# An attention and mixture-of-experts kernel: PE's lumps cut small and spread over the slots, q and k through the ring of shifted scores, straight code

## Chip, cores and metric

The kernel runs on one core of one Trainium2 chip. The metric is the device time of one execution in microseconds. Engines: PE is TensorE, DVE VectorE, ACT ScalarE, POOL GpSimd, SP SyncE (it only issues DMAs here).

## What is computed

One transformer layer on 16 batches of 256 tokens with 128 features, all in float32: attention with 16 heads of 8 features, then a mixture of 8 experts (top 2) and a shared expert.

```python
q, k, v = x @ Wq.T + bq, x @ Wk.T + bk, x @ Wv.T + bv      # 16 heads of 8
attn = softmax(q k^T / sqrt(8)) * head_mask
x = layernorm(x + (attn v) @ Wo.T + bo)
# routed: the two best of 8 experts per token, gates renormalised
y = shared(x) + sum over the two of gate_e * (gelu(x @ Wfc_e + bfc_e) @ Wproj_e + bproj_e)
out = layernorm(x + y)
```

## The kernel before

The attention (`build_attention`) is a pipeline over batches. In step t, PE, DVE, ACT, POOL and SP work on up to four batches at once: `new` = t, `now` = t-1, `late` = t-2, `last` = t-3. There are 19 steps; steps 0 to 3 and 14 to 18 are straight code, steps 4 to 13 run in a loop of five passes of two steps on each engine (`run_steps`, `Fori`). Steps 3 to 16 have work of all kinds but for the first and last batches' ends.

What a batch goes through. PE projects q and k (lines 588 and 589) into the PSUM bank `misc_ps`; ACT copies them out with the bias (370); POOL splits them in float16 parts (304, 306); SP writes the parts to rows in HBM (255 to 259) and reads them back, band by band, in `q_stack` and `k_stack` (225, 226). In the next step PE makes the scores of each head (527; 24 rows of the array, two tiles a head) in `s1_ps`, which has two places, and DVE takes the row maxima (443). POOL splits the maxima (292 to 296), PE turns them (569, in `misc_ps`), ACT copies them out (361), and SP adds them as two more rows to `q_stack` (215), in two halves of heads. In the step after, PE makes the shifted scores (543; 26 rows), two heads to a place of `st_ps`, which has two places, and ACT takes the exponentials into `probs` (354). `probs` has four buffers of a pair each. A quad (561) multiplies the probabilities of four heads with v: 8 float32 matmuls of 128 rows and 32 columns, which the trace shows as 16 instructions. One step later follow the copy out (380), the turning of `av` (622), the division by the sums and the head mask (465 to 472, DVE), the turning of the heads (628), the out projection (641), the addition of x (489), the statistics (493, 496), 1/sqrt on POOL (336 to 342), and the scaling to x1 on ACT (414).

A step of PE has 16 slots, one per head. In a slot PE issues four score matmuls: two tiles of `now`'s scores and two of `late`'s shifted scores. Between the slots stand the lumps: slot 0 q and k; slot 2 the maxima of the second half and quad 3 of `last`; slot 3 v; slot 5 the turning of `av`; slot 8 the heads; slot 11 the maxima of the first half; slot 13 the out projection; behind slots 6, 10 and 14 quads 0, 1 and 2 of `late`. All engines run their instructions in the written order; waits are on semaphores. In SP's order of a step, the second half's maxima come first, then x_t, x_in, the rows out, the stacks and the first half's maxima.

In step 18 PE turns rows for the routing stage between its slots (845). Then follow routing, the shared expert with the scattering of rows by POOL (886), the routed experts (39 blocks) and the last normalisation. Their loops take four tiles a pass; the first eight tiles are straight code.

Of the kernel before, what the change touches and what calls it, by code (L numbers as in the profile page):

```python
# [32 lines left out]
TURN_STEP = BATCHES + 2  # L33
TURNS = {1: (0, 1), 4: (2, 3), 7: (4, 5), 9: (6,)}
# [4 lines left out]
PASSED = [None]  # L39


class Batch:


    def __init__(self, u, c, back):
        self.half = u + (c - back) // 2
        self.par = (c - back) % 2
        self.n = self.half * 2 + self.par
        self.fixed = isinstance(u, int)

    def exists(self):
        return not self.fixed or 0 <= self.n < BATCHES

    def since(self, n):

        return not self.fixed or self.n >= n


def wait_first(eng, semaphore, value):


    eng.wait_ge(semaphore, value)
    if not isinstance(value, int):
        eng.sem_inc(PASSED[0], 1)


def run_steps(eng, step):

    for t in range(2 * FIRST_LOOP):
        step(t // 2, t % 2)  # L70
    with eng.Fori(FIRST_LOOP, FIRST_LOOP + LOOPS) as u:
        step(u, 0)
        step(u, 1)
    for t in range(2 * (FIRST_LOOP + LOOPS), BATCHES + 3):
        step(t // 2, t % 2)


def build_attention(nc, a):

    ctx = ExitStack()  # L80
    with ctx:
# [17 lines left out]
        wo = sb("wo", [D, D])  # L99
        bq = sb("bq", [D, 1])  # L100
# [3 lines left out]
        mask_row = sb("mask_row", [P, HEADS])  # L104
# [22 lines left out]
        probs = sb("probs", [P, 4, 2, TILES, SEQ])  # L127
        av = sb("av", [P, 2, SEQ])
        sum_inv = sb("sum_inv", [P, 2 * HEADS])
        sum_scale = sb("sum_scale", [P, 2 * HEADS])  # L130
# [6 lines left out]
        scaled_mean = sb("scaled_mean", [P, TILES])  # L137
        shift = sb("shift", [P, TILES])
# [3 lines left out]
        st_ps = ps("st_ps", [P, 2, 2, TILES, SEQ])  # L142
# [4 lines left out]
        misc16 = misc_ps[:].bitcast(F16)  # L147
# [13 lines left out]
        qk_projected = sem("qk_projected")  # L161
        qk_evacuated = sem("qk_evacuated")
# [9 lines left out]
        shifted_ready = sem("shifted_ready")  # L172
        exp_done = sem("exp_done")
# [18 lines left out]
        def _(sp):  # L192
            def load_xt(b):
                sp.dma_start(x_t[:, b.par], a["x_t"][:, bass.ds(b.n * SEQ, SEQ)]).then_inc(xt_in[b.par], 16)

            load_xt(Batch(0, 0, 0))
# [5 lines left out]
            sp.dma_start(mask_row[:], a["mask"].partition_broadcast(P)).then_inc(bcast_in, 16)  # L202
# [15 lines left out]
            def load_stacks(b, half):  # L218
                if b.since(2):

                    sp.wait_ge(shifted_ready, PAIRS * (b.n - 2) + (half + 1) * PAIRS // 2)
# [6 lines left out]
            def step(u, c):  # L228
                b = Batch(u, c, 2)
                if b.exists():  # L230
                    load_max(b, 1)
                b = Batch(u, c, -1)
                if b.exists():

                    if b.since(2):
                        sp.wait_ge(v_projected, b.n - 1)
                    load_xt(b)
                b = Batch(u, c, 2)
                if b.exists():
                    if b.since(2):  # L240
                        sp.wait_ge(xb_made, b.n - 1)
                    sp.dma_start(x_in[:, b.par], a["x"][bass.ds(b.n * SEQ, SEQ), :].rearrange("(t p) d -> p t d", p=P))\
                      .then_inc(x_loaded[b.par], 16)
                b = Batch(u, c, 0)
                if b.exists():


                    q_to = q_rows[b.par].rearrange("(r d) h t -> (d h) r t", r=TERMS)
                    k_to = k_rows[b.par].rearrange("(r d) h t -> (d h) r t", r=TERMS)
                    q_part, k_part = qk_parts[:, b.par, 0], qk_parts[:, b.par, 1]  # L250
                    if b.since(2):
                        for half in range(2):
                            sp.wait_ge(stacks_in[b.par][half], 64 * b.half)
                    sp.wait_ge(qk_split, 2 * b.n + 1)
                    sp.dma_start(q_to[:, 0:1], q_part[:, 0:1]).then_inc(rows_out[b.par], 16)
                    sp.dma_start(k_to[:, 2:3], k_part[:, 0:1]).then_inc(rows_out[b.par], 16)
                    sp.wait_ge(qk_split, 2 * b.n + 2)
                    sp.dma_start(q_to[:, 1:3], q_part[:, 0:2]).then_inc(rows_out[b.par], 16)
                    sp.dma_start(k_to[:, 0:2], k_part[:, 0:2]).then_inc(rows_out[b.par], 16)
                new, now = Batch(u, c, 0), Batch(u, c, 1)  # L260
# [7 lines left out]
                load_for_moe(sp, a, u, c)  # L268

            run_steps(sp, step)  # L270

        @block.gpsimd
        def _(pool):
# [9 lines left out]
            def split_max(b, half):  # L283
# [5 lines left out]
                wait_first(pool, max_done, HEADS * b.n + (half + 1) * HALF)  # L289
                if b.since(1):  # L290
# [17 lines left out]
            def step(u, c):  # L308
                b = Batch(u, c, 2)
                if b.exists():  # L310
                    split_max(b, 1)
# [1293 lines left out]
```

## Time and profile before

| | us |
|---|---|
| median of 3 runs | 655.3 |
| lowest, highest | 651.41, 659.56 |
| the profiled execution | 650.02 |
| its span | 648.3 |
| attention to the last out projection | about 334 |
| granted TensorE clock, mean of the span | 0.783 |

The profile is of one execution. Its span is the time from the first to the last instruction; the execution's own time is 1.7 us more. Times in the rows are from the span's start. The granted clock is 1.00 at 2.4 GHz and 0.50 at 1.2 GHz. Matmuls that run side by side on different rows or columns of the array, as a score and a shifted score or four matmuls of a quad, start within 0.01 us of each other, and PE's busy time counts them once. A matmul's duration holds its latency too, so two starts tell more than a duration.

### The profile page before, as it was taken

How to read it: one execution, taken by the hardware profiler on the slowest of the kernel's cores; microseconds unless marked ns; L12 is line 12 of the kernel's file. 1: busy time of each engine (PE TensorE's matmuls, PEld its weight loads, DVE VectorE, ACT ScalarE, POOL GpSimd, SP SyncE). 2: the span in 40 equal slices, each digit the busy share in tenths (PEclk: the TensorE clock that was granted, in tenths of full speed). 3: DMA queues.
4: the chain of work that ended last, by engine and by line, in shares of the span. 5: the costliest groups of instructions: out<-in, count | busy, mean ns of one | idle time of the engine just before them, and what ended most of it. 6: DMA issues, size and time to landing. Idle time of an engine off the chain costs nothing. (4 is left out here: it accounts for less than half of the span.)

```text
span 648.3 us, 15805 instructions
## 1 busy us (share of the span) xinstructions
PE 477.3 (74%) x5002; PEld 302.3 (47%) x5003; DVE 401.4 (62%) x871; ACT 306.2 (47%) x551; POOL 275.4 (42%) x398
## 2 busy tenths in 40 slices
PE   3898899988998989899961499800299999999000
PEld 2334344444344344434341399800188888888000
DVE  2757775666567576656558577600078888887066
ACT  1147755666556565644534477600054444443025
POOL 5203322323222232321024478877026677678366
PEclk9999975787578586855585599955599999999555
DMA  3222224242233423521205011111671011101093
GB/s 82 61 60 66 75 90 114 85 116 82 61 92 89 115 86 91 133 83 46 73 3 131 26 51 41 42 53 53 159 175 41 32 38 36 34 28 41 8 281 103
DMA packets 72502, 49.84 MB, mean 77 GB/s; under 512 B 9594, under 2 KB 65028, under 8 KB 72468
## 3 DMA queue, kind: packets, MB, share of 16 engines
q1 hardware_dynamic: 67924, 40.92, 23.2%
q0 software_dynamic: 4544, 8.47, 4.0%
q8 instruction: 20, 0.33, 0.2%
q14 instruction: 14, 0.11, 0.1%
HBM read 24.96 MB, written 22.95 MB: 74 GB/s over the span
## 5 line engine op out<-in xcount | busy, mean ns | idle before, releaser
L443 DVE TENSOR_REDUCE row_max<-s_ps 128x2 f32<-128x512 f32 x256 | 165.9, 684 | 98.0 <-PE s_ps L527 94.6
L354 ACT ACTIVATE probs<-st_ps 128x1024 f32<-128x1024 f32 x128 | 129.3, 1024 | 54.2 <-PE st_ps L543 53.4
L527 PE MATMUL s_ps<-k_stack,q_stack 24*128 24x256 f16 x512 | 113.9, 338 | 24.2 <-DVE row_max L443 11.4
L1306 POOL DMA_INDIRECT results<-gated,dest x78 | 89.2, 1144 | 64.1 <-DVE gated L1409 48.1
L1380 ACT ACTIVATE hid_r<-h_ps_r,bias 128x256 f32<-128x256 f32 x156 | 61.1, 474 | 114.7 <-PE h_ps_r L902 114.7
L543 PE MATMUL st_ps<-q_stack,k_stack 26*128 26x256 f16 x512 | 112.4, 339 | 0.4 <-ACT probs L354 0.4
L561 PE MATMUL av_ps<-probs,v_aug 128*32 128x256 f32 x1024 | 97.0, 513 | 0.0
L527 PEld LDWEIGHTS s_ps<-k_stack,q_stack 24*128 24x128 f16 x512 | 37.3, 104 | 101.5 <-DVE row_max L443 50.8
L886 POOL DMA_INDIRECT slots<-rows,slot_at x64 | 70.3, 1099 | 32.1 <-issue 18.9
L914 PE MATMUL y_ps_r<-w,hid_r 128*128 x312 | 59.0, 221 | 0.0
L915 PE MATMUL y_ps_r<-w,hid_r 128*128 x312 | 58.6, 219 | 0.0
L913 PE MATMUL y_ps_r<-w,hid_r 128*128 x312 | 58.1, 220 | 0.0
L292 POOL TENSOR_SCALAR max_scaled<-row_max 128x16 f32<-128x16 f32 x32 | 6.5, 205 | 114.0 <-DVE row_max L443 113.0
L1332 PE MATMUL t_ps<-ident_h,w_or_slots 128*128 128x128 f16 x156 | 17.4, 227 | 47.6 <-DMA w_or_slots<-slots 45.1
L561 PEld LDWEIGHTS av_ps<-probs,v_aug 128*32 128x32 f32 x1024 | 33.0, 134 | 35.5 <-issue 29.5
L1420 DVE SCALAR_TENSOR_TENSOR hid_r<-hid_r 128x1024 f16<-128x1024 f32 x39 | 48.1, 1232 | 1.3
L336 POOL TENSOR_SCALAR var_eps<-mean_var 128x2 f32<-128x2 f32 x16 | 3.5, 222 | 100.0 <-DVE mean_var L496 100.0
L900 PE MATMUL h_ps_r<-rows,w 128*128 128x256 f16 x156 | 43.6, 280 | 2.3 <-DVE rows L1399 2.3
L901 PE MATMUL h_ps_r<-rows,w 128*128 128x256 f16 x156 | 43.6, 279 | 0.0
L902 PE MATMUL h_ps_r<-rows,w 128*128 128x256 f16 x156 | 43.5, 279 | 0.0
L543 PEld LDWEIGHTS st_ps<-q_stack,k_stack 26*128 26x128 f16 x512 | 38.0, 106 | 8.0 <-issue 3.3
L1417 DVE TENSOR_SCALAR hid_r<-hid_r 128x1024 f16<-128x1024 f32 x39 | 27.1, 694 | 21.1 <-ACT hid_r L1380 19.9
(173 smaller groups left out, 1011.3 us busy)
## 6 DMA issues: line engine op xcount, KB each, us to landing
slots<-empty_row SPq DMA_DIRECT2D x6, 780.0 KB, 6.0
expert<-results SPq DMA_DIRECT2D x16, 256.0 KB, 5.1
w_or_slots<-slots SPq DMA_DIRECT2D x3, 1040.0 KB, 11.0
q_stack<-q_rows SPq DMA_DIRECT2D x64, 48.0 KB
k_stack<-k_rows SPq DMA_DIRECT2D x64, 48.0 KB
w_or_slots<-in_w_fc SPq DMA_DIRECT2D x9, 256.0 KB, 2.8
w_or_slots<-in_w_proj SPq DMA_DIRECT2D x9, 256.0 KB, 2.8
x_t<-in_x_t SPq DMA_DIRECT2D x16, 128.0 KB, 2.2
```

The costliest lines, as they stand in the source:

```text
L354: nc.scalar.activation(probs[:, p % 4], st_ps[:, p % 2], ACT.Exp, scale=SCORE_SCALE).then_inc(exp_done, 1)
L443: nc.vector.tensor_reduce(row_max[:, h], s1_ps[:, h % 2], AX_X, ALU.max, negate=True).then_inc(max_done, 1)
L527: mm = nc.tensor.matmul(s1_ps[:, h % 2, t], band_of(q_stack, b, h, TERM_ROWS)[:, t * P:(t + 1) * P], band_of(k_stack, b, h, TERM_ROWS), st ...
L543: mm = nc.tensor.matmul(st_ps[:, p % 2, n % 2, t], band_of(k_stack, b, h, rows)[:, t * P:(t + 1) * P], band_of(q_stack, b, h, rows), start ...
L561: mm = nc.tensor.matmul(av_ps[32 * j:32 * j + 32, r], v_aug[:, b.par, t, s * HALF + r * 4 + j], probs[:, (2 * n + j // 2) % 4, j % 2, t], ...
L886: nc.gpsimd.indirect_dma_start(out=a["slots"][:, :], out_offset=bass.IndirectOffsetOnAxis(ap=slot_at[:, k, t:t + 1], axis=0), in_=rows[:, ...
L913: nc.tensor.matmul(y_ps, h_hi[:, units], one_of(w16[:, 0], e, lo, hi), start=False, stop=False)
L914: nc.tensor.matmul(y_ps, h_hi[:, units], one_of(w16[:, 1], e, lo, hi), start=False, stop=False)
L915: mm = nc.tensor.matmul(y_ps, h_lo[:, units], one_of(w16[:, 0], e, lo, hi), start=False, stop=(c == CHUNKS - 1))
L1306: nc.gpsimd.indirect_dma_start(out=a["results"][:, :], out_offset=bass.IndirectOffsetOnAxis(ap=dest[:, t.buf, half:half + 1], axis=0), in_ ...
L1380: act_ = nc.scalar.activation(hid[:, t.buf % 2, cols], h_ps[:, t.buf % 2, cols], ACT.Gelu_apprx_tanh, scale=1.0 / UNIT, bias=bias[:, t.buf ...
L1420: nc.vector.scalar_tensor_tensor(out=hid16[:, t.buf, 1], in0=hid[:, t.buf % 2], scalar=X_UNIT, in1=hid16[:, t.buf, 0], op0=ALU.mult, op1=A ...
```

## The change

- A quad is cut in two half quads (4 matmuls each, one tile of probabilities). PE's lumps now stand: slot 0 k; 1 half quad 2b of `last`; 2 maxima, half quad 3a; 3 half quad 3b; 4 v; 6 turning of av; 7 and 8 quad 0; 10 maxima, 1a; 11 1b; 12 heads; 13 half quad 2a; 14 out projection; 15 q of the batch ahead. All stand ahead of the slot's scores.
- q and k are projected into the ring of two places that the shifted scores use; a batch's q and k take one place, and the ring has nine fillings a step.
- `probs` has six buffers; the exp of a pair waits for a quad one pair older than before.
- The head mask is multiplied once into `wo_masked`; the operation on `sum_scale` goes.
- x1 is scaled on POOL with (z - mean) * rstd; `scaled_mean`, `shift` and ACT's scaling go. The statistics of a batch are taken one step later, so there are 20 steps.
- SP sends the rows of q and k ahead of x_t and x_in.
- All loops, in the attention and behind it, are straight code; `wait_first` with its extra increments goes.

The diff, cut to its core:

```diff
+STEPS = BATCHES + 4
+PROBS = 6
-        with eng.Fori(FIRST_LOOP, FIRST_LOOP + LOOPS) as u: ...
+def run_steps(step):
+    for t in range(STEPS):
+        step(t)
+def ring_order():
+    at = {("qk", 0): 0}
+    for t in range(STEPS):
+        if Batch(t - 2).exists():
+            for p in range(PAIRS):
+                at["pair", t - 2, p] = len(at)
+        if Batch(t + 1).exists():
+            at["qk", t + 1] = len(at)
+    return at
...
 SP, step:
+                if late.exists():
+                    load_max(late, 1)
+                if new.exists():
+                    send_rows(new)
+                if ahead.exists():
+                    load_xt(ahead)
...
 POOL:
+            def make_x1(b):
...
+                nc.gpsimd.tensor_tensor(rstd[:], var_eps[:], minus_half[:], ALU.pow).then_inc(scale_done, 1)
+                pool.wait_ge(scale_done, 2 * b.n + 2)
+                for t in range(TILES):
+                    nc.gpsimd.tensor_scalar(x1_all[:, b.n * TILES + t], z[:, t], mean_var[:, t, 0:1], rstd[:, t:t + 1],
+                                            ALU.subtract, ALU.mult).then_inc(x1_made, 1)
+            # order: split_max(late, 1), split_qk(new), make_x1(gone), add_bias(last), split_max(now, 0)
 ACT:
-                if b.since(1) or p >= 4:
-                    act.wait_ge(quad_done, 4 * b.n + p // 2 - 1)
+                if n >= PROBS:
+                    act.wait_ge(quad_done, (n - PROBS) // 2 + 1)
+            # order: evacuate_qk(new), pair 0, max(late, 1), pair 1, av(last), v(now), pairs 2 3 4,
+            #        max(now, 0), pair 5, heads(last), pairs 6 7
 DVE:
+            # order: maximum 0, stats(gone), maximum 1, mean(gone), maxima 2 to 7, sums and division(last),
+            #        maxima 8 to 15, add_residual(last)
+            nc.vector.tensor_tensor(wo_masked[:], wo[:], mask_col[:].to_broadcast([D, D]), ALU.mult)
 PE:
+            def half_quad(b, n, t):
...
+                for j in range(4):
+                    mm = nc.tensor.matmul(av_ps[32 * j:32 * j + 32, r], v_aug[:, b.par, t, s * HALF + r * 4 + j],
+                                          probs[:, (PAIRS * b.n + 2 * n + j // 2) % PROBS, j % 2, t], start=(s == 1 and t == 0),
+                                          stop=(s == 0 and t == 1))
+            def project_q(b):
+                key = ("qk", b.n)
+                pe.wait_ge(xt_in[b.par], 16 * (b.half + 1))
+                if place[key] >= 2:
+                    pe.wait_ge(ring_emptied, filled(key) - 2)
+                nc.tensor.matmul(ring(key)[:, 0, 0], wq[:], x_t[:, b.par], start=True, stop=True)
+            def project_k(b):
+                nc.tensor.matmul(ring(("qk", b.n))[:, 0, 1], wk[:], x_t[:, b.par], start=True, stop=True).then_inc(ring_filled, 1)
...
+                    if slot == 0 and new.exists():
+                        project_k(new)
+                    if slot == 1 and last.exists():
+                        half_quad(last, 2, 1)
+                    if slot == 2 and late.exists():
+                        if gone.exists():
+                            pe.wait_ge(z_made, gone.n + 1)
...
+                        turn_max(late, 1)
+                    if slot in (2, 3) and last.exists():
+                        half_quad(last, 3, slot - 2)
...
+                    if slot in (7, 8) and late.exists():
+                        half_quad(late, 0, slot - 7)
...
+                    if slot == 14 and last.exists():
+                        project_out(last)
+                    if slot == 15 and ahead.exists():
+                        project_q(ahead)
 behind the attention:
-    with eng.Fori(2, loop_end) as u: ...
+    for s in range(steps):
+        step(s // 4, s % 4)
```

## Rows read from the trace of the kernel before

**Rows 1.** The page, part 1: busy us, share of the span and instructions.

```profile
PE 477.3 (74%) x5002; PEld 302.3 (47%) x5003; DVE 401.4 (62%) x871; ACT 306.2 (47%) x551; POOL 275.4 (42%) x398
```

**Rows 2.** Busy time by stretch: steps 3 to 16, routed experts. Columns: stretch, length, engines, clock, DMA.

```profile
46.90:308.60 261.70, 234.35 (x2072) 108.99 (x2071) 171.06 (x337) 155.47 (x248) 68.59 (x180) 0.74 0.32 89
...
470.00:602.00 132.00, 124.52 (x1619) 112.89 (x1617) 107.48 (x230) 61.10 (x156) 85.92 (x75) 0.99 0.18 52
```

**Rows 3.** Busy time by step: steps 4, 6 and 9 (PE, PEld, DVE, ACT, POOL, clock).

```profile
62.70:78.30 15.60, 12.99 (x148) 6.20 (x148) 11.91 (x25) 11.18 (x18) 4.64 (x14) 1.00 0.25 71
...
96.10:118.70 22.60, 21.75 (x151) 9.79 (x149) 12.42 (x24) 11.41 (x18) 5.02 (x13) 0.50 0.31 83
...
152.10:174.40 22.30, 20.41 (x151) 9.19 (x149) 12.53 (x25) 11.29 (x18) 5.62 (x15) 0.56 0.24 71
```

**Rows 4.** Busy time by stretch of one granted clock, four of sixteen.

```profile
49.00:89.90 40.90, 34.03 (x395) 16.11 (x395) 31.84 (x62) 29.43 (x48) 13.16 (x32) 1.00 0.29 85
89.90:120.70 30.80, 29.95 (x204) 13.64 (x197) 16.90 (x35) 15.51 (x24) 6.97 (x20) 0.50 0.26 71
...
154.80:175.30 20.50, 19.65 (x138) 9.02 (x139) 11.30 (x23) 9.55 (x15) 4.39 (x10) 0.50 0.23 68
...
270.80:328.90 58.10, 54.58 (x384) 24.43 (x382) 33.90 (x69) 29.36 (x43) 9.11 (x28) 0.50 0.28 78
```

**Rows 5.** Timeline of PE in step 6, half clock, to its end. Columns: start, us, what.

```profile
105.56 0.42 PE L543 MATMUL st_ps<-q_stack,k_stack 26*128 26x256 f16 x1
...
105.77 0.42 PE L543 MATMUL st_ps<-q_stack,k_stack 26*128 26x256 f16 x1
...
106.11 1.94 PE L561 MATMUL av_ps<-probs,v_aug 128*32 128x256 f32 x16
...
106.55 0.20 PEld L561 LDWEIGHTS av_ps<-probs,v_aug 128*32 128x32 f32 x4 [0.23 <-issue]
...
107.98 0.39 PE L527 MATMUL s_ps<-k_stack,q_stack 24*128 24x256 f16 x1
...
114.15 1.22 PE L641 MATMUL misc_ps<-wo,heads_t 128*128 128x128 f32 x4
115.30 0.39 PE L527 MATMUL s_ps<-k_stack,q_stack 24*128 24x256 f16 x1
...
116.27 1.94 PE L561 MATMUL av_ps<-probs,v_aug 128*32 128x256 f32 x16
...
118.67 1.22 PE L588 MATMUL misc_ps<-x_t,wq 128*128 128x256 f32 x2
...
120.68 0.28 PE L527 MATMUL s_ps<-k_stack,q_stack 24*128 24x256 f16 x1
```

**Rows 6.** Groups of instructions by line: busy us, mean ns, idle before.

```profile
L414 ACT ACTIVATE x_all<-z,shift,rstd 128x128 f32 (+1 forms) x32 | 13.9, 483 | 4.0 <-POOL shift L342 3.9
...
L304 POOL TENSOR_SCALAR qk_parts<-qk 128x512 f16<-128x512 f32 x16 | 9.9, 617 | 21.3 <-ACT qk L370 21.3
...
L292 POOL TENSOR_SCALAR max_scaled<-row_max 128x16 f32<-128x16 f32 x32 | 6.5, 205 | 114.0 <-DVE row_max L443 113.0 <-issue 0.9
```

**Rows 7.** Timeline of SP's DMA issues in step 4, full clock.

```profile
66.46 2.69 SPq L215 DMA_DIRECT2D q_stack<-max_t  x4
69.46 0.39 SPq L194 DMA_DIRECT2D x_t<-in_x_t  x1
...
70.80 0.33 SPq L255 DMA_DIRECT2D q_rows<-qk_parts  x1
...
75.85 2.72 SPq L215 DMA_DIRECT2D q_stack<-max_t  x4
```

**Rows 8.** Timeline of PE at slot 0 of step 15.

```profile
268.94 0.27 PE L527 MATMUL s_ps<-k_stack,q_stack 24*128 24x256 f16 x1 [1.70 <-DMA q_stack<-max_t]
```

**Rows 9.** Timeline of PE: the q projections of steps 2 and 4.

```profile
27.58 1.22 PE L588 MATMUL misc_ps<-x_t,wq 128*128 128x256 f32 x2
...
62.69 0.69 PE L588 MATMUL misc_ps<-x_t,wq 128*128 128x256 f32 x2
```

More of the change, by code:

```diff
@@ L36, with __init__ @@
 FIRST_LOOP, LOOPS = 2, 5
-PASSED = [None]
 class Batch:
[L45 to L49, printed above, removed]
-    def exists(self):
[L52 to L75, printed above, removed]
+    def __init__(self, n):
+        self.n = n
+        self.par = n % 2
+        self.half = n // 2
+    def exists(self):
+        return 0 <= self.n < BATCHES
+def ring_order():
[10 more added lines that the diff above has]
+        step(t)
 def build_attention(nc, a):
@@ new lines, in step @@
+            def step(t):
+                ahead, new, now, late = (Batch(t - back) for back in range(-1, 3))
+                if late.exists():
[4 more added lines that the diff above has]
+                    load_xt(ahead)
+                if late.exists():
+                    if late.n >= 2:
+                        sp.wait_ge(xb_made, late.n - 1)
+                    sp.dma_start(x_in[:, late.par], a["x"][late.n * SEQ:(late.n + 1) * SEQ, :].rearrange("(t p) d -> p t d", p=P))\
+                      .then_inc(x_loaded[late.par], 16)
@@ new lines, in step @@
+            def step(t):
+                new, now, late, last, gone = (Batch(t - back) for back in range(5))
+                if late.exists():
+                    split_max(late, 1)
+                if new.exists():
+                    split_qk(new)
+                    if new.n == 0:
+                        make_routing_constants(nc, pool, a)
+                if gone.exists():
+                    make_x1(gone)
+                if last.exists():
+                    add_bias(last)
+                if now.exists():
+                    split_max(now, 0)
@@ L566, in turn_max @@
-            def turn_max(b, half):
-                rows = MAX_PARTS * HALF * TILES
-                wait_first(pe, max_split, (2 * b.n + half) * 3 + 3)
-                nc.tensor.transpose(misc16[0:rows, 0:P], max_parts[:, half].rearrange("p r n -> p (r n)"), ident16[:])\
-                  .then_inc(max_turned, 1)
-            def step(u, c):
-                new, now, late, last = (Batch(u, c, back) for back in range(4))
-                turning = isinstance(u, int) and 2 * u + c == TURN_STEP
+                if t == 0:
+                    pe.wait_ge(ring_emptied, emptied(("pair", b.n, 2 * n + 1)))
+                    if n == 0:
+                        pe.wait_ge(v_evacuated, 2 * b.n + 2)
+                        if b.n >= 1:
+                            pe.wait_ge(av_evacuated, b.n)
+                        else:
+                            pe.wait_ge(bias_made, 1)
@@ L576, in step, with project_out @@
+            def project_out(b):
+                pe.wait_ge(heads_evacuated, b.n + 1)
+                for t in range(TILES):
+                    mm = nc.tensor.matmul(half_ps[:, t * D:(t + 1) * D], heads_t[:, t * P:(t + 1) * P], wo_masked[:],
+                                          start=True, stop=True)
+                mm.then_inc(y_ready, 1)
+            def step(t):
+                ahead, new, now, late, last, gone = (Batch(t - back) for back in range(-1, 5))
                 for slot in range(HEADS):
-                    if turning:
+                    if t == TURN_STEP:
@@ L604, in step @@
+                    if slot == 4 and now.exists():
+                        if now.n == 0:
+                            pe.wait_ge(weights_in, 64)
                         if late.exists():
                             pe.wait_ge(max_evacuated, 2 * late.n + 2)
[L606 to L610 removed]
@@ L611, in step @@
-                        mm.then_inc(v_projected, 1)
-                    if slot == 5 and last.exists():
+                        project_v(now)
+                    if slot == 6 and last.exists():
                         if now.exists():
```

504 lines of the change are left out of this document (218 added, 286 removed).

## The prediction

> **What bounds the kernel now.** I read the page's busy shares first, then the busy times by stage, by step of the attention, by stretch of one granted clock, and then single instructions. PE is the busiest engine and is busy for three quarters of the span [rows 1]. The change touches the attention above all, whose fourteen full steps (3 to 16) fill 46.9 to 308.6, 261.7 us [rows 2]. These steps do the same work and don't take the same time: 15.6 us at clock 1.00, 22.6 us at 0.50 [rows 3]. In the first PE is busy for 12.99 us, DVE 11.91 and ACT 11.18, so no engine is full; in the second PE is busy 21.75 of 22.6 and nothing else matters. The reader should see two kernels in one: a latency-bound one at 2.4 GHz and a PE-bound one at 1.2 GHz.
>
> How the steps are shared out follows from the stretches of one clock [rows 4] (sixteen of them from 5 us on). From 46.9 to 308.6 the full-clock ones add up to 122.6 us (7.9 steps of 15.6) and the half-clock ones to 139.1 us (6.2 steps of 22.6), which gives the 0.74 of [rows 2]. Ahead of 49 us the row's 1.00 isn't to be believed: a q projection took 1.22 us at 27.58 as it does at half clock, against 0.69 at 62.69 [rows 9]. The kernel starts at half clock.
>
> **What moves the clock here.** A full PE doesn't raise it: from 89.9 PE was busy 29.95 of 30.8 us at 0.50, from 270.8 it was busy 54.58 of 58.1 us and stayed at 0.50 [rows 4]. Each of the seven rises in the attention (49.0 to 253.8) comes in the first 7 us of a step. There the work on the whole array (128*128, or four 128*32 side by side) stands densest: quad 2 (116.27), one slot of scores, q and k without a break (118.67 to 120.68), then quad 3, v and the transposes; at 120.7 the clock rises [rows 4, 5]. The 58 us in which it never came back are the ones in which no q/k projection ran at half clock, since the last ran at 266.1. The falls (89.9, 137.7, 154.8, ..., 270.8) come behind scores on 24 or 26 of the 128 rows and a stall, as the 1.70 us at 268.94 [rows 8]. So whole-array work packed together goes ahead of a rise, and mere occupation doesn't bring one. This is read from when things happen; it isn't proven.
>
> **The change on PE, at half clock.** One pair of score matmuls takes 0.21 us (105.56 to 105.77), a slot of two pairs 0.43. A quad starts 0.13 us after the last pair has streamed (106.11 - 105.77 - 0.21), its four groups are 0.43 or 0.44 apart (106.11, 106.55), and the next scores start at 107.98, 0.16 us behind 4 x 0.43. A quad costs 1.71 + 0.29 = 2.00 us, 0.29 of it edges [rows 5]. A half quad costs 0.86 + 0.29 = 1.15. Eight for four quads: 8 x 1.15 - 4 x 2.00 = +1.2 us a step. The out projection costs 0.13 + (115.30 - 114.15) = 1.28; q and k together cost 0.13 + (120.68 - 118.67) = 2.14, and apart, in slots 15 and 0, 2 x 1.28: +0.4 us [rows 5]. Against that, stalls that lumps of 2 us cause shrink; the step has 0.85 us without PE busy [rows 3], of which I take 0.4 back. 22.6 + 1.6 - 0.4 = **23.8 us** per half-clock step. The bounds are 22.9 (edges half as dear, since the next weights may be loaded ahead) and 24.6 (no stall returned and an edge of 0.35).
>
> More important is the order. At half clock the new PE runs lump, slot of scores, lump, slot of scores from slot 13 to slot 4. Between two score slots stands at most 0.86 us of whole-array work, in 1.15 + 0.43 = 1.58 us. The old stretch that led to the rise at 120.7 had 1.71 (quad) + 1.71 (q and k) = 3.4 us of it in the 4.4 us from 116.27 to 120.68 [rows 5]. Nothing as dense is left anywhere: q has a slot of scores between itself and k, and every quad is cut. The start is no help either: step 0 has q, k and the small bias matmul together, as before, and that didn't raise the clock before [rows 9]. I therefore take it that the clock, which starts at 0.50, isn't raised before the turning step, where transposes of the routing stage run without scores.
>
> **The rest, part by part.** *x1 on POOL*: ACT loses 2 x 0.48 us a step (line 414); POOL gets two scalings of 128x128, between the 0.205 of 16 elements and the 0.617 of 512 [rows 6]; by length 0.30 each, 0.6 us, and loses two small ones of about 0.2. POOL is busy 4.6 to 5.6 us a step [rows 3]: hidden. Its queue holds split_max(now, 0) behind make_x1 and add_bias; both are done long before slot 8's maximum. The scaling gates DVE's next addition to z one step later: hidden. *Mask in the weights*: one DVE operation less a step, one 128x128 multiply once: DVE has over 10 us free at half clock. *Six probs buffers*: exps wait for a quad one pair older; only full-clock steps could gain. *q/k through the ring*: nine fillings a step in two places where there were eight; an ACT that is busy 11.4 of 22.6 us covers them. Its cost falls on full-clock steps, where a pair's scores wait for the evacuation of q and k (0.9 us); nothing to 0.5 us. *turn_max in slot 2* waits for the z of the batch before, now the last thing DVE does in a step; two slots and a k projection at half clock (over 2 us) cover 0.42 us of z. *SP*: rows go ahead of x_t and x_in. In a full-clock step SP issues the second half's maxima at 66.46, x_t at 69.46, rows at 70.80, and the next maxima, which slot 0 waits for, from 75.85 to 78.57 [rows 7]. Taking x_t and x_in out of that order shortens it by 70.80 - 69.46 = 1.3 us, so a **full-clock step** would go from 15.6 to 14.3, I say 14.4; at half clock it is slack. *Step 19*: the last batch's statistics come one step later, with nothing between; the ACT scaling (0.97) becomes 0.6 of POOL. -1 to +1. *Straight code*: behind 339 us PE in the routed stage is busy 124.52 of 132 us [rows 2], so loops and register arithmetic have little to give: 0 to -3, I take -1; more instructions to fetch, nothing in the steps that were already straight shows a cost: 0 to +3. Routing, shared expert, routed experts and the last normalisation are as before.
>
> **The sum.** Steps 3 to 16 at half clock: 14 x 23.8, less the q of step 15 and the q and k of step 16 (3 x 1.28), is 329.4 us against 261.7: **+67.7**. Steps 2, 17 and 18, at half clock before and after, have two, four and two lumps more: +2. Tail and code: -2. 650.0 of the profiled execution (span 648.3) becomes 718. The median of the runs lies 5.3 us above that execution; with it, **722**. Bounds by 22.9 and 24.6 a step: 705 to 735.
>
> **The rivals.**
> *The clock rises and stays (faster).* Place: any half-clock window that brings it up. From there the same evenness keeps it up: at 2.4 GHz a slot with a lump would last about 0.9 us, whole-array work comes in nearly every slot, and only slots 5 and 9 are left with scores alone. Price: 14 x 14.4 = 202 for 261.7, -60: 595. It pays for itself as soon as about 48% of the steps run at full clock (23.8 against 14.4, mean 18.7). For it: at full clock PE would be busier than the 12.99 of 15.6. Against it: it has to rise first, and a wait of 1.7 us for maxima at slot 0 would end it, with no way back.
> The Trainium skill, page "TensorE: Matmul & The Clock Gate", the section on the HAM clock gate, says of throttling that "the default state is throttled, and activity releases the throttle"; by that rule a PE that never idles would be released, and the time would be this rival's 595. The trace doesn't agree: 54.58 busy of 58.1 us at 0.50 [rows 4].
> I give it 0.14 from the start of the full steps and 0.12 for a rise on the way, 600 to 642.
> *Alternation as before (no change).* 7.9 x 14.4 + 6.2 x 23.8 = 261: gain at full clock and loss at half cancel, 655. So also if the DMA order eats the gain. For it: my reading rests on seven rises. 0.12.
> *My forecast*: 0.62.
>
> **How the numbers follow.** Two per cent is about what a measurement of this kernel tells from no change. Slower by more: 0.62. Within: 0.12. Faster: 0.14 + 0.12 = 0.26. The range goes to 735 above; below it has to reach into the faster cases until no more than 0.2 is left out: 615 leaves the 0.14 at 595 and a little of the way there. The likeliest case's own range is 705 to 735.
>
> **What would show it.** Right: granted clock 0.50 nearly throughout from 50 to about 395 us, steps near 23.8 us with PE busy over 95%, quads as x8 groups 1.15 us wide from scores to scores, DVE's waits for scores grown; DVE and ACT busy times less by about 3 and 15 us. Wrong: a stretch at 1.00 longer than 60 us. If steps are 14 to 15 us, the clock was what I misread; if half-clock steps are under 22.6, the edges were.

## The result and the profile after

The changed kernel takes 704.96 us (median of four runs, 704.37 to 705.75), the kernel before 657.43 on the same chip (651.41 to 660.08): a ratio of 1.0737, 95% interval 1.0655 to 1.082. The forecast was slower, 722 us. Ratios given with an interval leave out runs over 1.5% above the fastest run of their kernel, so they can differ a little from the quotient of the medians.

First the page of the changed kernel: busy time by engine, then the three rows in 40 slices that matter.

```profile
span 702.6 us, 14097 instructions
...
PE 559.1 (80%) x5002; PEld 303.0 (43%) x5002; DVE 403.5 (57%) x855; ACT 293.5 (42%) x519; POOL 285.9 (41%) x398
...
PE   3899999999999999999999616994007999999200
...
PEclk9999999999999999999999857998557999999755
```

Against [rows 1], PE is busy 82 us more with the same 5002 instructions. No work was added to it, so each instruction lasts longer. The groups by line say which (line, engine, operation, tile, count | busy us, mean ns | idle before):

```profile
L531 PE MATMUL s_ps<-k_stack,q_stack 24*128 24x256 f16 x512 | 147.2, 404 | 3.6 <-DVE row_max L437 1.9 <-issue 0.4
L547 PE MATMUL ring_ps<-q_stack,k_stack 26*128 26x256 f16 x512 | 146.6, 405 | 0.0
L565 PE MATMUL av_ps<-probs,v_aug 128*32 128x256 f32 x1024 | 138.8, 631 | 0.7 <-ACT probs L350 0.7
```

One score matmul is recorded with 404 ns on the mean. At half clock [rows 5] record 0.39 to 0.42 us, at full clock the traces record 0.27 or 0.28 (further down), and a mix of both had to give something between. So the scores ran at half clock throughout. The PEclk row prints 9 all the same: the first clock event in this trace stands at 391.0 us, and ahead of it the row shows full speed by default, as the prediction said of the first 49 us of the trace before [rows 9]. A reader who believed the row would look for the loss in the wrong place; durations decide.

Now the attention. Busy time of steps 3, 4, 5 and 14, and of steps 3 to 16 together (the clock column is that default); these answer to [rows 2, 3]:

```profile
47.90:71.00 23.10, 23.02 (x150) 8.07 (x148) 11.57 (x18) 10.43 (x16) 3.70 (x9) 1.00 0.16 48
71.00:94.10 23.10, 23.01 (x150) 8.07 (x148) 12.45 (x23) 10.44 (x16) 6.28 (x13) 1.00 0.17 47
94.10:117.20 23.10, 23.01 (x150) 8.07 (x148) 12.45 (x23) 10.44 (x16) 6.26 (x13) 1.00 0.24 70
302.20:325.30 23.10, 23.01 (x151) 8.06 (x149) 12.45 (x23) 10.44 (x16) 6.25 (x13) 1.00 0.31 82
47.90:368.20 320.30, 318.76 (x2074) 112.01 (x2076) 172.89 (x317) 145.24 (x222) 83.27 (x176) 1.00 0.27 74
```

From 47.90 to 325.26 each step takes 23.11 us, like a clock, with PE busy 23.01 of it. A kernel that alternated between latency-bound and PE-bound steps has become PE-bound in all of them. DVE and ACT have idle time for it: maxima wait 162.8 us for scores (94.6 in the page of before), the exps 193.8 us for theirs (53.4 before).

```profile
L437 DVE TENSOR_REDUCE row_max<-s_ps 128x2 f32<-128x512 f32 x256 | 173.0, 690 | 165.3 <-PE s_ps L531 162.8
L350 ACT ACTIVATE probs<-ring_ps 128x1024 f32<-128x1024 f32 x128 | 131.2, 1025 | 193.8 <-PE ring_ps L547 193.8
```

The order at half clock, slots 15 to 2 around the start of step 14 (start, us, what): q, k and two half quads, each with a slot of scores behind it. From the start of a lump to the next scores it is 1.3 us at most, here 1.02 to 1.30:

```profile
300.46 1.22 PE L581 MATMUL ring_ps<-x_t,wq 128*128 128x256 f32 x2
301.61 0.39 PE L531 MATMUL s_ps<-k_stack,q_stack 24*128 24x256 f16 x1
...
302.15 1.22 PE L584 MATMUL ring_ps<-x_t,wk 128*128 128x256 f32 x2
303.45 0.37 PE L531 MATMUL s_ps<-k_stack,q_stack 24*128 24x256 f16 x1
...
303.65 0.42 PE L547 MATMUL ring_ps<-q_stack,k_stack 26*128 26x256 f16 x1
303.99 1.08 PE L565 MATMUL av_ps<-probs,v_aug 128*32 128x256 f32 x8
305.01 0.39 PE L531 MATMUL s_ps<-k_stack,q_stack 24*128 24x256 f16 x1
...
305.55 1.13 PE L565 MATMUL av_ps<-probs,v_aug 128*32 128x256 f32 x8
306.62 0.39 PE L531 MATMUL s_ps<-k_stack,q_stack 24*128 24x256 f16 x1
```

Where the 54.3 us between the two spans lie: 1.0 ahead of step 3 (47.90 against 46.9), 58.6 in steps 3 to 16 (320.3 against 261.7), 3.2 from there to the first routing logit (at 402.20 against 339.35), and behind it -8.6.

### The profile page after: what moved, and what is told of

Its sections match the earlier page's. It is cut to its first block and busy times, and to the rows that moved or that the text cites. A ratio compares the mean times of both kernels' runs of the same rounds, so it can differ in the third digit from the quotient of the medians.

```text
span 702.6 us, 14097 instructions
## 1 busy us (share of the span) xinstructions
PE 559.1 (80%) x5002; PEld 303.0 (43%) x5002; DVE 403.5 (57%) x855; ACT 293.5 (42%) x519; POOL 285.9 (41%) x398
## 5 line engine op out<-in xcount | busy, mean ns | idle before, releaser
L437 DVE TENSOR_REDUCE row_max<-s_ps 128x2 f32<-128x512 f32 x256 | 173.0, 690 | 165.3 <-PE s_ps L531 162.8
L350 ACT ACTIVATE probs<-ring_ps 128x1024 f32<-128x1024 f32 x128 | 131.2, 1025 | 193.8 <-PE ring_ps L547 193.8
L531 PE MATMUL s_ps<-k_stack,q_stack 24*128 24x256 f16 x512 | 147.2, 404 | 3.6 <-DVE row_max L437 1.9
L547 PE MATMUL ring_ps<-q_stack,k_stack 26*128 26x256 f16 x512 | 146.6, 405 | 0.0
L565 PE MATMUL av_ps<-probs,v_aug 128*32 128x256 f32 x1024 | 138.8, 631 | 0.7 <-ACT probs L350 0.7
L1322 POOL DMA_INDIRECT results<-gated,dest x78 | 79.2, 1015 | 65.5 <-DVE gated L1423 52.4
L931 PE MATMUL y_ps_r<-w,hid_r 128*128 x312 | 58.2, 220 | 0.0
L932 PE MATMUL y_ps_r<-w,hid_r 128*128 x312 | 58.0, 219 | 0.0
L930 PE MATMUL y_ps_r<-w,hid_r 128*128 x312 | 57.7, 220 | 0.0
L565 PEld LDWEIGHTS av_ps<-probs,v_aug 128*32 128x32 f32 x1024 | 27.6, 142 | 41.3 <-issue 27.4
L547 PEld LDWEIGHTS ring_ps<-q_stack,k_stack 26*128 26x128 f16 x512 | 38.8, 112 | 7.9 <-issue 6.0
L1431 DVE TENSOR_SCALAR hid_r<-hid_r 128x1024 f16<-128x1024 f32 x39 | 27.1, 694 | 15.1 <-ACT hid_r L1394 15.1
L1409 DVE COPY bias<-b_units 128x4 f32 x39 | 7.1, 182 | 47.4 <-issue 47.4
```

Of the source, the lines that this page charges most:

```text
L350: nc.scalar.activation(probs[:, n % PROBS], ring(key), ACT.Exp, scale=SCORE_SCALE).then_inc(ring_emptied, 1)
L437: nc.vector.tensor_reduce(row_max[:, h], s1_ps[:, h % 2], AX_X, ALU.max, negate=True).then_inc(max_done, 1)
L531: mm = nc.tensor.matmul(s1_ps[:, h % 2, t], band_of(q_stack, b, h, TERM_ROWS)[:, t * P:(t + 1) * P], band_of(k_stack, b, h, TERM_ROWS), st ...
L547: mm = nc.tensor.matmul(ring(("pair", b.n, p))[:, n % 2, t], band_of(k_stack, b, h, rows)[:, t * P:(t + 1) * P], band_of(q_stack, b, h, ro ...
L565: mm = nc.tensor.matmul(av_ps[32 * j:32 * j + 32, r], v_aug[:, b.par, t, s * HALF + r * 4 + j], probs[:, (PAIRS * b.n + 2 * n + j // 2) % ...
L930: nc.tensor.matmul(y_ps, h_hi[:, units], one_of(w16[:, 0], e, lo, hi), start=False, stop=False)
```

## The experiments

Theories. **Order**: the sequence of PE's work decides whether the clock rises; whole-array work packed together goes ahead of a rise, and the new order has none. **Mere size**: the half quads' and ring's edges simply cost PE time. **Ring or waits**: the new dependences, not the clock, hold the steps. Each kernel below is set against runs of the kernel before ("before" for short) on its own chip.

**A burst of whole-array work.** Eight extra projections into a scratch tile, once, in step 3 ahead of the turning of the maxima:

```diff
+                        if t == 3:
+                            for _ in range(8):
+                                nc.tensor.matmul(misc_ps[:, 0:SEQ], wq[:], x_t[:, new.par], start=True, stop=True)
                         turn_max(late, 1)
```

> The kernel after, with eight extra 128x128 float32 matmuls (6.8 us at half clock, result unused) once, in step 3 ahead of the turning of the maxima. Theory (the clock starts at half and the evenly spread lumps never bring it up, while nothing else is wrong with the new order): the clock rises during or right behind the burst, and from there the same evenness keeps it up; steps of 14 to 15 us instead of 23.1, about 705 + 7 - 13 x 8.5 = 600 us; if a stall at slot 0 brings it down once, it is stuck again and the time is between 610 and 700. Rival (the new order costs PE time by itself, by its edges and waits): the burst adds its 7 us, 712 us.

Measured: median 697.19 us (three runs at 697.04 to 697.35, one at 656.54), before 661.59. The clock rose at 53.4 us, 2 us into the burst, which is 4.72 us long by its timeline, and 338 us earlier than in the changed kernel. It stayed up for 34.1 us, until 87.5, then was at half until 384.5. The burst, then the whole stretch at full clock, the one full step in it, and a later step at half (same columns as the tables of busy time before):

```profile
51.33 4.72 PE L633 MATMUL misc_ps<-x_t,wq 128*128 128x256 f32 x16
```

```profile
53.40:87.50 34.10, 28.68 (x301) 12.69 (x303) 22.72 (x41) 19.41 (x31) 7.56 (x19) 1.00 0.22 62
69.58:85.72 16.14, 13.43 (x151) 5.42 (x149) 12.23 (x23) 10.21 (x16) 6.30 (x13) 1.00 0.24 69
110.00:133.10 23.10, 23.01 (x152) 8.06 (x148) 12.44 (x23) 10.43 (x17) 6.27 (x14) 0.50 0.31 82
```

So half clock was no fault of the waits: with the clock up, the same order runs a step in 16.14 us instead of 23.11. But it is not the prediction's 14.4, and it doesn't hold the clock: the 600 us of the expectation were missed, and its other case, a fall that leaves the kernel stuck (610 to 700), came about. The fall came behind two waits on ACT, 0.27 us ahead of q and 0.61 us at the start of the next step:

```profile
84.79 0.67 PE L581 MATMUL ring_ps<-x_t,wq 128*128 128x256 f32 x2 [0.27 <-ACT probs L350]
87.02 0.26 PE L531 MATMUL s_ps<-k_stack,q_stack 24*128 24x256 f16 x1 [0.61 <-ACT probs L350]
...
87.34 0.97 PE L565 MATMUL av_ps<-probs,v_aug 128*32 128x256 f32 x8
```

The same two waits stand one step earlier (at 68.66 and 70.89) with no fall behind them, and PE was never idle for longer than 0.79 us while the clock was up. So the waits alone don't explain the fall. The run of 656.54 has no trace; its mean granted clock is 0.782 where the other three have 0.693. In it the clock stayed up longer or came back, so the order isn't a certain lock once the clock has moved.

**The same burst on 24 rows.** In the same place 32 matmuls of the scores' shape, 24 of the 128 rows, results unused:

```diff
+                        if t == 3:
+                            for _ in range(32):
+                                nc.tensor.matmul(misc_ps[:, 0:SEQ], q_stack[0:TERM_ROWS, now.par, 0, 0:P],
+                                                 k_stack[0:TERM_ROWS, now.par, 0], start=True, stop=True)
                         turn_max(late, 1)
```

> The same place and the same length of burst, but of 32 matmuls on 24 of the 128 rows (float16, 0.21 us each at half clock, result unused). Theory (whole-array work goes ahead of a rise, occupation doesn't): the clock stays at half, 705 + 7 = 712 us. Rival (any uninterrupted run of matmuls releases the clock): the same as the burst on the whole array, near 600.

Measured: 712.02 us (710.89 and 713.16), 1.0818 of before (1.0669 to 1.0967). First clock event at 397.8, routing at 408.93, 6.7 us later than in the changed kernel, which is about the burst itself:

```profile
51.23 7.03 PE L633 MATMUL misc_ps<-k_stack,q_stack 24*128 24x256 f16 x32
```

PE was occupied without a break for 7.0 us and nothing rose; 4.7 us on all rows raised it. PE is occupied in both, in the second even longer. But the two bursts differ in more than the rows: the first is float32, the second float16. The trace of the changed kernel answers this further on, in the routed experts. There PE ran float16 matmuls of the same width, on all 128 rows, from 531.05 on at half clock, and the clock rose at 534.35:

```profile
531.05 0.39 PE L917 MATMUL h_ps_r<-rows,w 128*128 128x256 f16 x1 [1.00 <-DVE rows L1413]
...
534.00 0.42 PE L917 MATMUL h_ps_r<-rows,w 128*128 128x256 f16 x1
534.22 0.34 PE L918 MATMUL h_ps_r<-rows,w 128*128 128x256 f16 x1
534.39 0.27 PE L919 MATMUL h_ps_r<-rows,w 128*128 128x256 f16 x1
```

So float16 work goes ahead of a rise too when it fills all rows, and the type isn't what held the second burst back. Bursts of one type on more and on fewer rows, in one place, were not run.

**Lumps packed again, the rest of the change kept.** Quads whole in slots 2, 7, 10 and 13, q beside k in slot 0:

```diff
                     if slot == 0 and new.exists():
+                        if new.n >= 1:
+                            project_q(new)
                         project_k(new)
-                    if slot == 1 and last.exists():
-                        half_quad(last, 2, 1)
-                    if slot in (2, 3) and last.exists():
-                        half_quad(last, 3, slot - 2)
+                    if slot == 2 and last.exists():
+                        half_quad(last, 3, 0)
+                        half_quad(last, 3, 1)
... quads 0, 1 and 2 likewise, whole in slots 7, 10, 13
-                    if slot == 15 and ahead.exists():
-                        project_q(ahead)
```

> The kernel after with PE's lumps packed as before: quads whole (slots 2, 7, 10, 13), q next to k in slot 0; ring, six buffers, x1 on GpSimd and straight code stay. Theory: the clock rises again at the beginning of steps and falls in between, 640 to 660 us. Rival (another part of the change costs the 47 us): 690 to 705, less the edges alone.

Measured: 634.27 us (630.41 to 639.91), 0.9617 of before (0.9512 to 0.9722), better than the 640 to 660 expected. It beats both kernels. The trace is of the longest run, 639.91. The clock rises nine times in the attention (74.3 to 326.9) and once stays up for 75.1 us. Two full-clock steps:

```profile
163.45:178.60 15.15, 12.37 (x149) 5.99 (x148) 11.77 (x24) 10.19 (x17) 6.27 (x13) 1.00 0.36 106
193.76:208.90 15.14, 12.36 (x149) 6.00 (x148) 11.76 (x24) 10.18 (x17) 6.28 (x13) 1.00 0.37 106
```

The first rise, at 74.3, came inside the quad of slot 2, behind q and k without a break and two slots of scores; the next scores already take 0.28 us instead of 0.39:

```profile
69.82 1.22 PE L581 MATMUL ring_ps<-x_t,wq 128*128 128x256 f32 x2
70.83 1.06 PE L584 MATMUL ring_ps<-x_t,wk 128*128 128x256 f32 x2
71.83 0.39 PE L531 MATMUL s_ps<-k_stack,q_stack 24*128 24x256 f16 x1
...
72.80 1.83 PE L565 MATMUL av_ps<-probs,v_aug 128*32 128x256 f32 x16
74.56 0.28 PE L531 MATMUL s_ps<-k_stack,q_stack 24*128 24x256 f16 x1
```

Six probs buffers, the ring, the mask in the weights, x1 on POOL and the DMA order are all still in this kernel. None of them by itself is the loss.

**Quads whole, q still in slot 15.**

```diff
 (against the packed kernel)
-                        if new.n >= 1:
-                            project_q(new)
                         project_k(new)
...
+                    if slot == 15 and ahead.exists():
+                        project_q(ahead)
```

> Quads whole again, but q still in slot 15 and k in slot 0. Theory: the edges of the half quads go (-1.2 us a half-clock step, 690 us at least), and the 1.7 us of a whole quad bring the clock up now and then: 650 to 690. Rival (only q and k side by side bring it up): 23.1 - 1.2 = 21.9 us a step throughout, 690 us.

Measured: 678.48 us (673.16 and 683.80) against 661.59. Seven short rises, 3.4 to 23.9 us. The half-clock step takes 22.98 us, hardly less than 23.11: the edges of four cuts that were saved come back as waits, for PE is busy only 21.77 of 23.00 us:

```profile
69.60:92.60 23.00, 21.77 (x152) 9.26 (x148) 12.05 (x23) 10.43 (x16) 6.29 (x13) 0.50 0.17 48
```

**q beside k, quads in halves.** The changed kernel with one lump moved:

```diff
                     if slot == 0 and new.exists():
+                        if new.n >= 1:
+                            project_q(new)
                         project_k(new)
...
-                    if slot == 15 and ahead.exists():
-                        project_q(ahead)
```

> The kernel after with q back in slot 0 beside k; the quads stay in halves. Theory: q and k together are 1.7 us of whole-array work without scores between, so the clock rises in some steps, less often than with whole quads as well: 640 to 680 us, half-clock steps 0.4 us shorter than 23.1. Rival (the cut quads alone keep the clock down): 14 x 0.4 less than 705, 698.

Measured: 693.84 us (679.61 to 700.04) against 709.22 for before; on this chip the stages behind the attention take about 60 us longer (from the first logit to the end 361 us against 300, 40 us of it up to the first routed transposition, 164 against 124), so ratios are compared. That of the medians is 0.978 here, but only one run of four is near the fastest, so it is rough. Routing begins at 328.71. The clock was up from 72.2 to 198.5 without a break. One full-clock step and two at half:

```profile
85.74:100.83 15.09, 13.12 (x149) 5.50 (x148) 12.14 (x24) 10.32 (x17) 6.29 (x13) 1.00 0.37 108
212.41:234.94 22.53, 22.53 (x149) 8.38 (x148) 12.36 (x24) 10.43 (x17) 6.27 (x13) 0.50 0.25 73
234.94:257.47 22.53, 22.53 (x150) 8.39 (x149) 12.35 (x24) 10.43 (x17) 6.27 (x13) 0.50 0.32 83
```

**Half quads alone, in the kernel before** (each quad's two tiles in two neighbouring slots, nothing else):

```diff
-                    if slot == 2 and last.exists():
-                        quad(last, 3)
+                    if slot in (2, 3) and last.exists():
+                        quad(last, 3, slot - 2)
...
-                        if slot in (6, 10, 14):
-                            quad(late, (slot - 6) // 4)
+                        if slot in (6, 7, 10, 11, 14, 15):
+                            quad(late, (slot - 6) // 4, (slot - 6) % 4)
```

> The kernel before with its quads in halves and nothing else (slots 2 and 3, and behind slots 6, 7, 10, 11, 14, 15); q and k stay together in slot 0. Theory: less whole-array work in one piece, so fewer rises, and 1.2 us more of edges in a half-clock step: 665 to 690. Rival (halves feed DVE more evenly and are worth it): 640 to 655.

Measured: 744.79 us (737.39 to 752.13), 1.0445 of before (1.0335 to 1.0555). In the trace, of the longest of the four runs, half clock held from 80.9 to 207.2 us, with steps like these:

```profile
80.90:207.20 126.30, 120.74 (x788) 47.55 (x785) 67.03 (x130) 60.94 (x96) 27.19 (x72) 0.50 0.26 71
88.30:111.90 23.60, 22.56 (x149) 8.87 (x148) 12.53 (x24) 11.42 (x18) 4.91 (x13) 0.50 0.23 68
```

Cutting the quads is enough to lose 4%, though q stands beside k here as well. Part of it is size and not clock: the half-clock step takes 23.60 us against 22.6, up to 1.0 us a step. So neither cut alone explains the result, and "q beside k" alone doesn't save it: where the other lumps stand around it counts too.

**Straight code alone, in the kernel before**, behind the attention, nothing else:

```diff
-    for s in range(8):
-        step(s // 4, s % 4)
-    with eng.Fori(2, loop_end) as u: ...
+    for s in range(steps):
+        step(s // 4, s % 4)
... the loops of PE and DVE over the routed blocks likewise
```

> The kernel before with straight code behind the attention alone; the attention keeps its loop. From the two traces the stages behind the attention took 309.0 us before and 300.4 after. If straight code did it: 8 us less than before in the same runs. If the indirect transfers or the clock of that execution did it: no difference.

Measured: 709.02 us against 709.22, 0.9974 (0.9909 to 1.0038): none of the 8 us, on the chip with the long stages. Read by its expectation this clears the straight code; the same kernel on a chip of the other kind, below, says otherwise.

**A hybrid**: q beside k, quads 2 and 3 whole, quad 0 cut between slots 7 and 9, quad 1 between 10 and 11.

```diff
 (against q beside k)
-                    if slot == 1 and last.exists():
-                        half_quad(last, 2, 1)
-                    if slot in (2, 3) and last.exists():
-                        half_quad(last, 3, slot - 2)
+                    if slot == 2 and last.exists():
+                        half_quad(last, 3, 0)
+                        half_quad(last, 3, 1)
-                    if slot in (7, 8) and late.exists():
-                        half_quad(late, 0, slot - 7)
+                    if slot in (7, 9) and late.exists():
+                        half_quad(late, 0, (slot - 7) // 2)
                     if slot == 13 and late.exists():
                         half_quad(late, 2, 0)
+                        half_quad(late, 2, 1)
```

> From the fully packed order (634 us): q and k together, quads 2 and 3 whole, but quad 0 in halves in slots 7 and 9 and quad 1 in halves in slots 10 and 11, because the packed order's falls came 7 to 11 us behind a step's start, behind slots of scores alone. Theory: rises as often, falls less often: 615 to 632 us. Rival (any cut makes rises rarer and that costs more): 640 to 665.

Measured: 699.90 us (689.90 to 700.89) against 709.22. Stretches at full clock of 3.4 to 23.9 us that alternate with falls; routing at 339.01. The theory (615 to 632 us, which is 0.93 to 0.96 of the 661.59 of the first experiments) failed: by medians the hybrid is 0.987 of before, no better than q beside k alone. The reading of rises and falls didn't tell beforehand which order keeps the clock up.

**The three orders side by side.** The changed kernel, q beside k, and the packed kernel once more, unaltered, on one chip (again one with the long stages):

> The changed kernel as it is, on the chip of the two runs below, so that the three stand side by side. If the order of the work sets the clock (my theory), attention steps of 23.1 us without a rise again, the routing stage begins about 402 us behind the start on a chip like the first, ratio to before 1.07. If the missing rise were an accident of one chip or one session, a stretch of full clock in the attention and under 690 us.

> q's projection beside k's in slot 0, the rest of the change as it is. By my theory this one move brings rises in the attention that the changed kernel lacks: on a chip like the first, router at about 330 to 340, ratio to before 0.96 to 0.98 and 0.90 to 0.92 of the changed kernel. By the rival, that the half quads alone keep the clock down, under 0.97 of the changed kernel isn't reached.

> Whole quads in slots 2, 7, 10 and 13 and q beside k in slot 0, the rest of the change as it is. 0.96 of before as in its first run. Against q beside k with half quads: if whole quads add rises, 5 to 15 us less than it; if the lump of q and k is what counts, the two are within 5 us of each other.

Measured, with before at 714.83:

| kernel | median us | of before (95%) | routing begins at |
|---|---|---|---|
| changed | 771.21 | 1.0805 (1.0723 to 1.0886) | 403.32 |
| q beside k | 703.18 | 0.9895 (0.9802 to 0.9988) | 330.88 |
| packed | 690.43 | 0.9682 (0.9596 to 0.9769) | 323.70 |

The changed kernel has its first clock event at 393.7 us, as on the first chip, so the lock is the kernel's and not a chip's. One projection moved by one slot gives 68 us back. The packed order is 12.8 us better than that by medians, but one of its four runs took 709.29, so I call the sign likely and the size open. Of before, q beside k reaches 0.9895 where 0.96 to 0.98 was expected; the 0.90 to 0.92 of the changed kernel holds (0.912).

Taken together, with the rest of the change kept and each on its own chip: packed 0.962 and 0.968 of before, only the quads cut 0.978 and 0.990, only q apart from k 1.026 (two runs), both 1.074 and 1.081. Here moving q away from k is the dearer of the two cuts.

**Straight code once more**, the same kernel as above:

> The kernel before with straight code behind the attention and nothing else, once more. The five profiles of straight code from the chip on which the shared expert takes about 50 us have the routed experts, from the first transposition to the last projection, at 128.2 to 128.8 us; the loops of before had 135.8. If the straight code is the cause of that difference, 128 to 129 us in this profile and 0.985 to 0.99 of before, where the chip is of that kind; if the attention's change is the cause, 135 to 136 us and no difference. On a chip of the other kind (shared expert about 130 us) I expect about 150 us either way, and nothing is told apart.

Measured: 649.28 us against 657.46, 0.9897 (0.9823 to 0.9972). This chip has the short stages. The routed experts, from the first transposition to the last projection: of the kernel before (loops), of the changed kernel, and of this one:

```profile
463.00:599.00 136.00, 128.19 (x1638) 115.30 (x1638) 107.95 (x233) 61.10 (x156) 83.53 (x73) 0.97 0.24 66
```

```profile
526.70:655.30 128.60, 122.66 (x1638) 113.56 (x1638) 106.75 (x233) 61.22 (x156) 74.44 (x74) 0.97 0.26 72
```

```profile
466.20:594.20 128.00, 122.42 (x1637) 113.48 (x1638) 106.84 (x233) 61.22 (x156) 73.76 (x74) 0.97 0.26 72
```

The 128 us come with the straight code and not with the attention's change. From the first logit to the end of the span this kernel takes 300.7 us, the changed one 300.4, the kernel before 309.0: nearly all of the -8.6 us is the straight code's.

## Why the prediction was right, and where its sums were off

**The likeliest case came about as argued.** The clock starts at half and isn't raised before the turning step: first event at 391.0, where the prediction put "about 395". PE is busy 23.01 of 23.11 us. The time itself, 704.96, lies at the very edge of that case's own range (705 to 735), since the errors below nearly all run one way. The share of the full-clock steps was the whole question, and the reading of [rows 4, 5], which was marked as unproven, has since been tested: the bursts on all rows and on 24 rows, and the three orders. What is shown is that in this kernel the order decides and that occupation doesn't. What exactly raises or keeps the clock isn't: half quads beside q and k keep it up for 126.3 us in one kernel and down for 126.3 us in another. Nor are the falls explained.

On the Trainium skill, page "TensorE: Matmul & The Clock Gate", Part 1, the text says that a monitor sets the clock "based on how busy the PE has been recently". The runs don't agree if busy means occupied: 318.76 of 320.3 us at half clock, and a rise only where all rows worked.

**The half-clock step: 23.11 us, forecast 23.8** (bounds 22.9 to 24.6). Its two parts were both a little off. PE's busy time grew from 21.75 to 23.01, by 1.26 where 1.6 was summed. The price of a half quad isn't the reason: on the chip it is (303.99 - 303.65 - 0.21) + (305.01 - 303.99) = 1.15 us, as summed. Where the other 0.34 went stays open. And the idle 0.85 us of the old step shrank to 0.10: 0.75 came back where I took 0.4. Even work is better at removing stalls than I allowed; it just isn't worth it at half clock. Steps 3 to 16 took 320.3 us, forecast 329.4: +58.6 for +67.7. In the terms of the sum: 718 was forecast for a profiled execution that took 704.4; 9.1 of the difference are these steps, 6.6 the straight code (below), and the steps around them took 2.2 more than summed. The 5.3 us from profile to median of the kernel before had no counterpart: the changed kernel's runs lie within 1.4 us. So the theory of mere size is answered too: cutting and moving the lumps costs 0.5 us a half-clock step (23.11 against 22.6 before; 22.98 with whole quads, 22.53 with q beside k), at most 14 x 0.5 = 7 us of the 58.6. In the kernel before the cut quads cost 1.0 (23.60).

**Steps ahead and behind.** +2 for steps 2, 17 and 18; measured 1.0 ahead of step 3 and 3.2 between step 16 and the logits, with step 19 in it: +4.2, and step 19 had been given -1 to +1.

**Straight code.** -1 was taken from 0 to -3; it is -8.6 in the traces, on chips of the one kind. The step of the argument that failed is that PE in the routed stage "is busy 124.52 of 132 us [rows 2], so loops and register arithmetic have little to give". In these 136 us PE's busy time fell from 128.19 to 122.66 with the same count of matmuls: busy time itself held something the loops cost. On the chip with long stages the routed experts take 149.93 us straight, and 150.85 in the one trace with loops there (that of the half quads alone); why the gain isn't seen on that chip is open. What it is that overlaps better in straight code isn't shown.

**The full-clock step: 14.4 forecast, wrong.** The changed order has 16.14, where before had 15.6. The maxima's DMAs, which slot 0 waited for, hold neither the full step of the burst nor the one of q beside k any more. But the term was too large: 1.3 us was what SP's issues would shrink by, while PE's wait for them in the step that was priced, step 4 of before, is 0.68, and no more could come back:

```profile
64.50 0.28 PE L527 MATMUL s_ps<-k_stack,q_stack 24*128 24x256 f16 x1 [0.68 <-DMA q_stack<-max_t]
```

In its place stand, in the step of the burst, ACT (0.79 us for `v_aug`, 0.45 and 0.61 for `probs`, 0.27 ahead of q) and POOL (0.59 for `max_parts`). The 0.61 and the 0.27 stand where q and k, one ring place filled in two different slots, meet the exps; with q beside k neither is in the trace and the step is 15.09. I had given this "nothing to 0.5"; it is about 1. These are the waits of the full-clock step of q beside k, to compare:

```profile
91.48 0.66 PE L596 MATMUL misc_ps<-ident,av 128*128 128x128 f32 x4 [0.79 <-ACT v_aug L373]
...
95.12 0.22 PE L573 MATMUL misc_ps<-ident,max_parts 128*32 128x128 f16 x1 [0.59 <-POOL max_parts L290]
...
98.13 0.64 PE L565 MATMUL av_ps<-probs,v_aug 128*32 128x256 f32 x8 [0.45 <-ACT probs L350]
```

**The faster rival.** It would have paid for itself from 54% of the steps at full clock on, (23.8 - 18.7) / (23.8 - 14.4), not from 48%. Its price was too high: with 15.1 to 16.1 us a step, fourteen full-clock steps take 211 to 225 us for 261.7, so 36 to 50 less and not 60. Its first half, a clock that rises by itself, didn't happen: both traces of the changed kernel are without it, and their eight runs lie within 0.7% on either chip. Its second half, that evenness keeps the clock up, holds in part: the changed order lost the clock after 34.1 us with no wait longer than 0.79 us, so the 1.7 us that was argued isn't needed; but q beside k kept it for 126.3 and 139.9 us, which no stretch of before reached in the attention.

**POOL, ACT and DVE.** ACT's busy time fell by 12.7 us (forecast about 15), POOL's rose by 10.5, and PE is idle only 0.10 us of a half-clock step: hidden, as said. DVE's was to fall by about 3 us and rose by 2.1, from 401.4 to 403.5. The operation on `sum_scale`, 3.1 us in the kernel before, is gone as forecast, but the 256 maxima are busy 173.0 us where they were 165.9. At half clock that costs nothing.

## What to carry to other kernels

Look first at which clock a stretch ran at, by the duration of one known instruction rather than by the clock row, and count steps per clock: 7.9 steps that took 15.6 us and now take the half-clock time of 22.6 make about 55 of the 58.6 us, while every cost of edges and waits together was about 1 us a step or less. When a change spreads TensorE's dense work evenly, ask what will still raise the clock, and run the order, since the rule behind it isn't known; packing the work, whole quads and q beside k, was worth 10% of the changed kernel and made the rest of the change a gain (0.96 of before). And keep a change's harmless parts apart: the straight code's 1% was there all the time, hidden under the loss.

## What the runs showed of the hardware that I had not expected

- A clock event row that begins only at 391.0 us: everything ahead of a trace's first event prints as full speed, 390 us of half clock here.
- 7.0 us of unbroken float16 matmuls on 24 rows don't raise the clock; 4.7 us of float32 on 128 rows do, already 2 us in, and float16 on 128 rows go ahead of a rise as well (534.35 us in the changed kernel).
- Two kinds of chips for the same kernel behind the attention: the stretch from first logit to first routed transposition takes 124 to 125 us on some and 163 to 166 us on others (kernels with loops and with straight code alike), with PE's idle time in the shared expert's projections put down to "issue", 0.0 us on one kind, 8 to 13 us a line in the changed kernel on the other. The cause isn't known. The attention doesn't differ: 402.20 and 403.32 us to the first logit.
